# Exponentials of two heads in one ScalarE instruction, with each pair of score banks side by side

## The reference, cut to what matters

```python
sim = jnp.einsum('bhnd,bhmd->bhnm', q, k) * DH ** (-0.5)
a = jax.nn.softmax(sim, axis=-1)
o = jnp.einsum('bhnm,bhmd->bhnd', a, v)
```

## Time and profile before

| what | value |
|---|---|
| three runs | 5939.23, 5964.02, 5966.58 us; median 5964.02 |
| the profiled execution | 5934.54 us, its span 5932.8 us |
| busy in the span | PE 91%, DVE 74%, ACT 57%, POOL 43% |
| mean granted PE clock | 0.955 of full |

### The profile page before, as it was taken

The page is one execution under the profiler, slowest core; times in us unless marked ns, Lnnn a source line. Parts: engine busy times, 40 slices in busy tenths (PEclk is TensorE's granted clock), DMA queues, the critical chain, the costliest instruction groups (busy, mean ns, idle before and its releaser), DMA issues. The chain is left out here.

```text
span 5932.8 us, 167110 instructions
## 1 busy us (share of the span) xinstructions
PE 5411.6 (91%) x66584; PEld 3112.1 (52%) x66584; DVE 4361.4 (74%) x6682; ACT 3379.4 (57%) x7674; POOL 2532.9 (43%) x2193
## 2 busy tenths in 40 slices
PE   5899999999998999999899899999989999999967
PEld 4554555545455455555545456455554545555442
DVE  6888776667888867576887886667788787767633
ACT  3455566565565566656455565665546556665634
POOL 2643544444343444544444344445434445444420
PEclk9999999999999999999999999999989999999975
DMA  4010010101001000010101101010100100101000
GB/s 105 12 40 16 15 29 14 32 12 40 18 17 43 14 26 19 22 24 17 43 13 32 25 14 33 11 34 14 36 21 14 38 17 19 25 14 31 10 17 6
DMA packets 282358, 145.85 MB, mean 25 GB/s; under 512 B 151517, under 2 KB 266813, under 8 KB 281470
## 3 DMA queue, kind: packets, MB, share of 16 engines
q1 hardware_dynamic: 281598, 135.17, 9.5%
HBM read 112.39 MB, written 3.01 MB: 19 GB/s over the span
## 5 line engine op out<-in xcount | busy, mean ns | idle before, releaser
L2032 ACT ACTIVATE probs<-ring 128x512 f32<-128x512 f32 (+1 forms) x4096 | 2084.0, 571 | 1245.9 <-PE ring L1535 1234.8
L2394 DVE TENSOR_REDUCE max_part<-ring 128x2 f32<-128x800 f32 (+2 forms) x2304 | 2257.5, 1009 | 687.2 <-PE ring L1535 678.1
L1511 POOL TENSOR_TENSOR weight_sum<-weight_sum,probs 128x512 f32<-128x512 f32 (+1 forms) x1408 | 1812.7, 1287 | 208.6 <-ACT probs L2032 68.4
L1511 POOL TENSOR_TENSOR weight_sum<-probs 128x512 f32<-128x512 f32 x256 | 331.6, 1295 | 2169.5 <-ACT probs L2032 1639.7
L1535 PE MATMUL o_acc<-probs,region 128*64 128x256 f32 (+1 forms) x6656 | 894.8, 389 | 3.4 <-issue 2.2
L1535 PE MATMUL ring<-qop,region 64*128 64x256 f16 x9984 | 790.4, 274 | 23.5 <-ACT probs L2032 6.9
L1535 PEld LDWEIGHTS ring<-qop,region 64*128 64x128 f16 x9984 | 454.3, 96 | 247.1 <-issue 114.4
L1535 PEld LDWEIGHTS o_acc<-probs,region 128*64 128x64 f32 (+1 forms) x6656 | 415.2, 136 | 280.7 <-issue 120.7
L1535 PE MATMUL ring<-shift_q,shift_k 64*128 64x256 f16 (+1 forms) x3840 | 535.1, 273 | 0.0
L2418 DVE RECIPROCAL o_inv<-ring 128x256 f32<-128x256 f32 x256 | 447.7, 1749 | 116.1 <-PE ring L1535 115.9
L1535 PE MATMUL o_acc<-probs,x_nv 128*32 128x256 f32 x6656 | 483.4, 407 | 27.6 <-ACT probs L2032 26.7
(11 more groups left out here) (191 smaller groups left out, 6935.7 us busy)
## 6 DMA issues: line engine op xcount, KB each, us to landing
stage<-in_wide SPq DMA_DIRECT2D x448, 64.0 KB, 2.0
nk<-x_nk SPq DMA_DIRECT2D x768, 25.0 KB
wo_stage<-in_wide SPq DMA_DIRECT2D x32, 512.0 KB, 4.0
ff_w<-in_ff_w SPq DMA_DIRECT2D x48, 256.0 KB, 3.0
stage<-in_wide SPq DMA_DIRECT2D x64, 128.0 KB, 2.6
v_stage<-in_wide SPq DMA_DIRECT2D x128, 64.0 KB, 1.9
ff_w<-in_ff_w SPq DMA_DIRECT2D x16, 512.0 KB, 3.6
v_stage<-kv_split SPq DMA_DIRECT2D x128, 48.0 KB, 1.7
```

The source lines that it names most:

```text
L1511: pool.tensor_tensor(total, before, probs[0:rows_, (un.chunk + k) % PROBS, :], ALU.add)\
L2032: act.activation(to, src, ACT.Exp, scale=t.scale).then_inc(exp_done.sem, 1)
L2394: dve.tensor_reduce(dst, src, AX.X, ALU.max).then_inc(*release(one))
```

## The change

The two chunks of a pair of heads become one ACT instruction: it waits for both (they were always signalled together), reads banks b and b+1 as one operand, writes both heads' places in probs, and adds 2 to exp_done. In the planner only the even chunks get an exp part, with an assumed duration of 0.96 us for a full pair and 0.6 us for the last one; values and POOL's additions depend on every second chunk; a pair of scores must take neighbouring banks, by the same choice as the maxima, and may not be issued when no two neighbours are free; both banks come free together. Because durations and banks enter the planner, the order of all engines is planned anew. The dependencies in values() are otherwise only rewritten.

```diff
@@ scores
+        if g % 2:
+            return
...
-        deps = [("PE", ("scores", g - g % 2))]
+        deps = [("PE", ("scores", g))]
         if g >= PROBS:
             deps += self.chunk_parts(g - PROBS)
-        self.part("ACT", "exp", due, one, 0.58 if tiles == 2 else 0.38, deps)
+        self.part("ACT", "exp", due, one, 0.96 if tiles == 2 else 0.6, deps)
@@ values
-        deps = [("ACT", ("scores", un.chunk + c)) for c in t.chunks_of(pair)]
+        deps = exps = [("ACT", ("scores", un.chunk + c)) for c in t.chunks_of(pair)[::2]]
@@ run
+        def paired(what):
+            return what[0] == "scores" or is_max(what)
...
-            if is_max(what):
+            if paired(what):
                 r = min(side_by_side(), key=lambda r: beside(r) + beside(r + 1))
                 found = [r, r + 1]
...
-                        if len(banks) < takes(what) or is_max(what) and not side_by_side():
+                        if len(banks) < takes(what) or paired(what) and not side_by_side():
...
-                        owner[("ACT", ("scores", g)), r] = r, "scores"
+                        owner[("ACT", what), r] = r, "scores"
@@ emptied
-            return exp_done.sem, exp_done.at(un.n, c + 1)
+            return exp_done.sem, exp_done.at(un.n, c // 2 * 2 + 2)
@@ exps
-                    act.wait_ge(scores_full.sem, scores_full.at(n, c + 1))
+                    act.wait_ge(scores_full.sem, scores_full.at(n, c + 2))
...
-                    src = ring[0:r, score_bank(g), 0:nt * N].rearrange("p (m q) -> p m q", m=nt)
+                    b = score_bank(g)
+                    src = ring[0:r, b:b + 2, 0:nt * N].rearrange("p h (m q) -> p h m q", m=nt)
                     if t.wide:
                         first = (un.chunk + 2 * pair) % PROBS
-                        to = probs[0:r, first:first + nt, h * N:(h + 1) * N]
+                        to = probs[0:r, first:first + nt, :].rearrange("p m (h q) -> p h m q", h=2)
                     else:
-                        to = probs[0:r, g % PROBS, 0:nt * N].rearrange("p (m q) -> p m q", m=nt)
-                    act.activation(to, src, ACT.Exp, scale=t.scale).then_inc(exp_done.sem, 1)
+                        to = probs[0:r, g % PROBS:g % PROBS + 2, 0:nt * N].rearrange("p h (m q) -> p h m q", m=nt)
+                    act.activation(to, src, ACT.Exp, scale=t.scale).then_inc(exp_done.sem, 2)
```

More of the change, by code:

```diff
@@ L717, in scores @@
         tiles = len(t.tiles(c // t.heads))
[L718 to L724, removed]
-        deps = [("PE", ("scores", g - g % 2))]
+        if g % 2:
+            return
+        deps = []
+        if c == 0:
+            deps.append(("ACT", ("job", n, t.shift_job)))
+            if t.wide:
+                deps.append(("DVE", ("job", n, t.last_low)))
+        self.part("PE", "scores", due, one, (0.45 if t.wide else 0.12) * tiles, deps, 0.25)
+        deps = [("PE", ("scores", g))]
         if g >= PROBS:
             deps += self.chunk_parts(g - PROBS)
-        self.part("ACT", "exp", due, one, 0.58 if tiles == 2 else 0.38, deps)
+        self.part("ACT", "exp", due, one, 0.96 if tiles == 2 else 0.6, deps)
     def values(self, due, one):
@@ L733, in values @@
         t = un.t
-        deps = [("ACT", ("scores", un.chunk + c)) for c in t.chunks_of(pair)]
+        deps = exps = [("ACT", ("scores", un.chunk + c)) for c in t.chunks_of(pair)[::2]]
         if pair == 0:
             if t.wide:
-                deps.append(("ACT", ("job", n, t.last_val)))
+                deps = deps + [("ACT", ("job", n, t.last_val))]
             elif un.p == 0:
-                deps += [("ACT", ("pre", t.sub, un.u, m)) for m in of_kind(t.sub, "val")]
+                deps = deps + [("ACT", ("pre", t.sub, un.u, m)) for m in of_kind(t.sub, "val")]
             if n:
-                deps.append(("ACT", ("close", n - 1)))
+                deps = deps + [("ACT", ("close", n - 1))]
         tiles = len(t.tiles(pair))
@@ L746, in values @@
                 old = self.wide[un.wide_at - 1]
-                deps = [*deps[:t.chunks_of(0)[-1] + 1], ("PE", ("job", old.n, old.t.sum_job))]
+                exps = [*exps, ("PE", ("job", old.n, old.t.sum_job))]
             adds = t.adds(pair) - (t.adds(pair - 1) if pair else 0)
-            self.part("POOL", "add", due, one, 1.3 * adds, deps)
+            self.part("POOL", "add", due, one, 1.3 * adds, exps)
     def close(self, due, one):
@@ L2022, in exps @@
                             act.wait_ge(weight_step.sem, weight_step.at(old.n, old.t.adds(pair)))
-                    pair, h = divmod(c, t.heads)
+                    pair = c // t.heads
                     tiles = t.tiles(pair)
                     r, nt = t.rows(tiles[0]), len(tiles)
-                    src = ring[0:r, score_bank(g), 0:nt * N].rearrange("p (m q) -> p m q", m=nt)
+                    b = score_bank(g)
+                    src = ring[0:r, b:b + 2, 0:nt * N].rearrange("p h (m q) -> p h m q", m=nt)
                     if t.wide:
                         first = (un.chunk + 2 * pair) % PROBS
-                        to = probs[0:r, first:first + nt, h * N:(h + 1) * N]
+                        to = probs[0:r, first:first + nt, :].rearrange("p m (h q) -> p h m q", h=2)
                     else:
-                        to = probs[0:r, g % PROBS, 0:nt * N].rearrange("p (m q) -> p m q", m=nt)
-                    act.activation(to, src, ACT.Exp, scale=t.scale).then_inc(exp_done.sem, 1)
+                        to = probs[0:r, g % PROBS:g % PROBS + 2, 0:nt * N].rearrange("p h (m q) -> p h m q", m=nt)
+                    act.activation(to, src, ACT.Exp, scale=t.scale).then_inc(exp_done.sem, 2)
                 def close(n):
```

## The result

The changed kernel took 6114.99 us (median of 4 runs, 6112.66 to 6119.32) against 5954.52 us for the kernel before beside it (5939.23 to 5966.58): a ratio of 1.0279, with a 95% interval of 1.0259 to 1.0299. It is slower by 2.8%. The forecast was 5975 us with a range from 5890 to 6045, so the prediction was wrong.

A forecast was written before the change was run, and what follows sets the result against it. PE was taken to bound the kernel, busy 5411.6 of 5932.8 us. Terms -12 + 12 + 11 + 0 = +11 us on the median of 5964 gave 5975 us, range 5890 to 6045.

The forecast's parts named there:

- Part 1: ACT's fused exponential: each pair ends 0.055 us sooner, shortening PE's 225 waits for exponentials, -12 us.
- Rival D: On ACT: the fused pair takes 1.08 us or more, sum +23 to +48; no chance of its own.
- Part 2: Ring banks: the first head's bank comes free 0.43 us later for one-bank jobs that wait, +12 us.
- Part 3: PE before scores: pairs now need two free neighbours of seven banks, +11 us.
- the upper figure: PE before scores: +46 us if score pairs came to wait for neighbouring banks as maxima do.
- rival B: Ring banks: the neighbour rule delays scores and maxima, +46 to +93 us, taken as +62, 6026 us; chance 0.31.
- Part 4: All engines' orders planned anew with 0.96 us where 1.03 is true: between +34 and -62 us, taken as 0.
- its mark of 115 us idle before scores: PE's idle time before the products of scores: 115 us or more would show that the bank rule bites.
- the 490 to 560: PE's total idle time in us; the forecast is wrong if it leaves this range.
- C: PE's clock: more small waits lower the mean to 0.93, about 142 us more busy time, 6117 us; chance 0.05.
- A: Planned order: denser plan removes half of PE's 123 us of waits for exponentials, -74 us, 5890 us; chance 0.28.

The follow-up runs named there:

- e1: Changed kernel with its plan, banks and waits, but each pair's exponentials as two instructions again: 6131.8 us, ratio 1.0279.
- e13: Kernel before, plan and instructions unchanged, but reuse of a score bank waits for both exponentials of its pair: 6161.4 us, ratio 1.0330.
- e17: Kernel before with both banks of a score pair released late, known to the planner; two instructions, no neighbour rule: 6072.2 us, ratio 1.0172.
- e18: Kernel before with the late release known to the planner, and 0.57 us for 0.58 as planned price of an exponential: 6036.6 us, ratio 1.0118.
- e7: Changed kernel with 0.97 us for 0.96 as the planner's price of a full pair, a second draw of its order: 6130.0 us, ratio 1.0299.
- e2: Kernel before with only the rule that score pairs take neighbouring banks; two instructions, banks freed one by one, old price: 6105.3 us, ratio 1.0235.
- e14: Kernel before with only the neighbour rule, and 1.14 us for 1.16 as the planner's price of a full pair: 6131.2 us, ratio 1.0271.
- e9: Kernel before, but score pairs take neighbouring banks when some are free and any two otherwise, nothing held back: 5997.5 us, ratio 1.0065.
- e3: Kernel before with only the planner's price of a full pair lowered to 0.96 us from 1.16: 6008.7 us, ratio 1.0079.
- e6: Kernel before with only the planner's price of a full pair raised to 1.18 us from 1.16: 5996.4 us, ratio 1.0084.
- e15: Kernel before, plan unchanged, with one more small ScalarE instruction of some 0.2 us in the whole program: 5958.9 us, ratio 0.9991.
- e5: Kernel before with only the planner's price of a full pair lowered to 1.12 us from 1.16: 5968.1 us, ratio 1.0019.
- e12: Kernel before with 6 banks in the ring in place of 7: 6213.6 us, ratio 1.0434.
- e10: Changed kernel with the planner's old price of 1.16 us for a full pair, 0.76 for the last one: 6070.4 us, ratio 1.0195.
- e4: Kernel before with only the planner's price of a full pair lowered to 1.14 us from 1.16: 6024.3 us, ratio 1.0093.

## Why the prediction was wrong, step by step

**Part 1, the instruction: right in size, worth nothing.** 1.024 us against 1.025 worked out, 0.590 for the short pair against 0.60, and 122 us less on ACT against 113. By the Trainium skill's "ScalarE: Activation LUTs", section "What ACT_TABLE_LOAD costs", it would be, as an estimate, 186 + 853 = 1039 ns; the trace has 1024, 15 ns less. The 12 us on PE were not seen: e1 and the changed kernel have one ratio, to 0.3% either way, and PE idle for 622 and 623 us. Rival D falls with this too.

**Part 2, the first bank's late release: mis-sized many times over.** The prediction said "I take a third, +12 us" and "if the planner fills them all with other work, 0", with 36 at the upper end. Measured: 198 us where the plan doesn't know of it (e13), and 107 and 71 us where it does (e17, e18), a new draw of the order included. The changed kernel's plan knows of it. What it adds there, on top of the rule, isn't shown: the changed kernel, e7 and e1 stand at 1.0279 to 1.0299, e2 and e14 at 1.0235 and 1.0271. The error was to count the waits that already ended on an exponential (168, half of them of that kind). With the later release there are 487 - 168 = 319 more, at places where the bank had come free in time. The mean length of a wait hardly moved (0.50 to 0.56 us).

**Part 3, the rule: the step that failed and carries most of the loss.** The mechanism was named rightly and its size was too small by far. "A quarter of the upper figure, +11 us" stood for it. e2 and e14 give 2.4 and 2.7% for the rule alone, 1.7 to 2.0% above the mean draw, which is some 100 to 120 us. The row to go by was there: scores came to wait as maxima do, 55 ns a pair (113.2 / 2048) where the maxima's 57 had been set as the upper figure, +43.5 us. What the sum left out were the maxima themselves, +52 us (rival B had 47 of them), and the values, +35 us, for which B had words but no price. The part of the maxima is there in e9 as well (169 us for 130) and cost no more than a draw. "PE has other work ready most times" was an assumption without a row; at run time the order of this kernel's queue is fixed and can't reach for that work, and in the plan the idle time elsewhere fell by only 29 us (274.3 to 245.4).

**Part 4, the new order: taken as 0 and not given a width.** It is 0.2 to 0.9% by e3 to e6, 0.7% or some 41 us in the mean. With the 110 us of the rule (mean of e2 and e14 over the mean draw) that is, as an estimate, 151 of the 160 us between the medians, where the sum had 11 for both. For a kernel whose order comes out of a greedy plan this term belongs in every sum.

**The rivals.** B happened, and its mark of 115 us idle before scores was met but for 2 us (113.2). Its price of 6026 us, 6057 at most, covered idle time only: 46 to 93 us against the 102 measured. PE's total idle time, 623 us, is outside the 490 to 560 that were to bear the forecast out. C came on top of it instead of in its place: its own sign, a clock under 0.945 with the same instruction counts and more busy time, is there (0.939, +53 to +80 us). C's sum of 6117 us is within 2 us of the result, and that is a coincidence: it stood for a clock of 0.93 with 142 us more busy time and 11 us of all else, and what came was 0.939 with 53 to 80 and 98 to 102. The Trainium skill's "TensorE: Matmul & The Clock Gate", section "A second HAM failure mode: psum-queue depth-cycling", ties short idle gaps in a cycle through PSUM banks to a clock that swings. The runs agree in direction and show no cause: the profiles with PE idle for over 570 us have 0.935 to 0.946, before and e15 with 521 and 525 have 0.955 and 0.949, but the other executions of before go from 0.942 to 0.956, and e5 has 549 us idle and 0.955. Treating B and C as separate cases was the mistake in the range: in every profile of a kernel with the rule, more waiting came together with a lower clock than in both profiles of the order of before. A had nothing for it: the idle time before o_acc's products with values was 79 us, not under 20.

**Rule and late release together.** Against the mean draw of 1.0069 the rule alone makes about 1.8% (mean of e2 and e14, 1.0253), the planned late release 0.8% (mean of e17 and e18, 1.0145), both 2.2% (1.0289, changed and e7). That the two don't add up to 2.6% would fit that both ask for the same thing, bank time, but 0.4% is inside the scatter of the draws and isn't shown. By the yardstick of e12, a bank is 1/7 of the bank time and 4.3%. The late release holds 2048 banks for 0.43 us longer, 881 us or 2.1% of 7 x 5933; at e12's rate, 0.021 x 7 x 4.3%, that is an estimate of 0.6%, near the 0.8 measured, though each of the two carries draws of up to 0.9%. Whether the price at which the exponentials were planned has a part in the loss stays open (e10), as does why e3 to e6 all lie above before.

## What to carry to other kernels

When instructions are merged, first ask what the first of them used to release early, and count its waiters by slack, not by the waits that exist: here banks held 0.43 us longer, unplanned, cost 198 us although ACT was idle for 43% of the time. An allocation rule should be priced by its nearest twin in the trace, for everything that shares the pool and what waits behind it (scores, maxima and values), with room for a lower granted clock, and by the planner's own end with the durations left as they are: it said +104 and +80 us for the rule (e2, e14) and -4 to +53 for new orders without it (e4 to e6), before anything ran. Before a change of a few per cent in a kernel with a planned order is believed, plan the old kernel anew two or three times by a meaningless change of a price; here that alone moved the time by up to 0.9%.

## What the runs showed of the hardware that was not expected

A third to nearly half of the time that the changed kernel lost showed as busy time, in products whose number and shapes were the same: 80 of 182 us against the profile with a granted clock of 0.955, 53 of 152 against the one with 0.949, and 0.939 in the changed kernel. And among kernels that differ in nothing but the order of their work, e3 to e6, the clock of the profiled execution went with its time: 0.955 at 5962 us (e5), 0.946 at 6015 (e6), 0.944 at 6024 (e3), 0.943 at 6027 (e4), with PE idle for 544 to 556 us in all four. It moves without any change of the program too: executions of before ran from 5937 us at 0.956 to 5998 us at 0.942, about as far as a new order moves the median. What makes the clock hold or fall, in an order or from one execution to the next, wasn't tried.
